# Graph network on one core: the softmax layers' edge loop keeps node columns, and W1 is applied in the node stage

## What is computed

```python
def _genconv(x, src, dst, W1, b1, g, be, W2, b2):
    msg = jax.nn.relu(x[src]) + EPS_MSG
    out = _softmax_aggregate(msg, dst, n) + x      # weights exp(msg), normalised per dst
    h = out @ W1 + b1                              # 128 -> 256
    mu = h.mean(axis=0)
    var = h.var(axis=0)                            # over all nodes
    h = (h - mu) * jax.lax.rsqrt(var + EPS_BN) * g + be
    h = jax.nn.relu(h)
    return h @ W2 + b2                             # 256 -> 128
```

## Time and profile before

| what | value |
|---|---|
| time, median of 3 runs | 6036.46 us (6026.17 to 6037.29) |
| span of the profiled execution | 6114.5 us (no time of its own is given beside it) |
| mean granted clock of TensorE | 0.846 |
| busy: PE, PEld, DVE, ACT, POOL | 69%, 58%, 39%, 31%, 55% |
| edge loops of layers 0, 1, 2 | 1324.60, 1299.00, 1246.00 us |
| stretch ahead of each loop | 68.40, 65.00, 67.00 us |
| node phase and table stores, layers 0, 1 | 66.00, 65.00 us |

### The profile page before, as it was taken

The page is one execution under the profiler, slowest core; times in us unless marked ns, Lnnn a source line. Parts: engine busy times, 40 slices in busy tenths (PEclk is TensorE's granted clock), DMA queues, the critical chain, the costliest instruction groups (busy, mean ns, idle before and its releaser), DMA issues.

```text
span 6114.5 us, 110249 instructions
## 1 busy us (share of the span) xinstructions
PE 4222.2 (69%) x26763; PEld 3555.3 (58%) x26763; DVE 2375.0 (39%) x6918; ACT 1871.9 (31%) x5164; POOL 3344.9 (55%) x3446
## 2 busy tenths in 40 slices
PE   2777777777677777777565555555556877777777
PEld 1666676766466666666455555555444655655555
DVE  3233333334333333333422222222533555555555
ACT  1222222222333333333321121111333444444445
POOL 1556665554366666666256666666135555555551
PEclk9888888888798888888777777777768989999999
DMA  2122222221233333333211111111134444444442
GB/s 69 51 61 62 61 61 61 61 62 44 59 104 105 104 103 104 103 105 104 61 36 43 43 42 43 43 43 44 52 93 122 124 116 123 121 118 123 118 122 73
DMA packets 389331, 487.68 MB, mean 80 GB/s; under 512 B 131848, under 2 KB 282106, under 8 KB 389224
## 3 DMA queue, kind: packets, MB, share of 16 engines
q0 software_dynamic: 119808, 245.58, 16.1%
q1 hardware_dynamic: 263161, 237.73, 12.8%
q10 hardware_dynamic: 6255, 3.20, 0.2%
HBM read 402.97 MB, written 83.21 MB: 80 GB/s over the span
## 4 chain that ended last, share of the span: by engine, by line
PE 21%; another core or an unknown queue 20%; issue 16%; ACT 7%; DVE 5%; DVEq 3%; ACTq 2%; DMA 1%; SPq 1%; PEldq 0%
PE ps L966 7%; PE ps L950 2%; DVEq L808 2%; PE ps L1422 1%; ACTq L808 1%; PE ps L1391 1%; PE ps L1410 1%; DVE xT L1496 1%; ACT work L896 1%; PE ps L1439 1%; PE ps L1428 1%; ACT work L1457 1%; ACT xT L1469 1%; PE ps L1152 1%
## 5 line engine op out<-in xcount | busy, mean ns | idle before, releaser
L782 POOL DMA_INDIRECT ring<-msg_table,idx_ring x2496 | 2437.6, 977 | 1669.2 <-issue 806.2
L966 PE MATMUL ps<-onehot,ring 128*128 128x128 f32 x9984 | 1542.0, 313 | 421.8 <-issue 378.0
L966 PEld LDWEIGHTS ps<-onehot,ring 128*128 128x128 f32 x9984 | 1423.3, 225 | 503.5 <-issue 449.5
L879 ACT ACTIVATE acc<-ps,b 128x42 f32 x1248 | 300.7, 292 | 2904.6 <-DMA starts<-in_dst 1871.2
L782 POOL DMA_INDIRECT ring<-h_table,idx_ring x832 | 831.0, 999 | 613.5 <-issue 205.9
L950 PE MATMUL ps<-work,W 128*128 128x128 f32 x2496 | 470.3, 317 | 299.1 <-DVE work L1024 179.0
L950 PEld LDWEIGHTS ps<-work,W 128*128 128x128 f32 x2496 | 415.3, 226 | 350.9 <-DVE work L1024 158.0
L992 DVE SCALAR_TENSOR_TENSOR ring<-ring 128x512 f32<-128x512 f32 x624 | 404.2, 648 | 449.3 <-ACT ring L884 324.6
L884 ACT ACTIVATE ring<-ring,negc 128x512 f32<-128x512 f32 x624 | 448.5, 719 | 0.0
L1017 DVE TENSOR_TENSOR work<-work,ps 128x84 f32<-128x84 f32 x624 | 151.6, 243 | 716.0 <-DMA msg_table<-ring 347.6
L1422 PE MATMUL ps<-work,few 128*128 128x512 f32 x416 | 245.1, 672 | 205.0 <-ACT work L1474 174.7
(11 more groups left out here) (193 smaller groups left out, 5658.2 us busy)
## 6 DMA issues: line engine op xcount, KB each, us to landing
e_few<-spare SPq DMA_DIRECT2D x208, 256.0 KB
xT<-e_few SPq DMA_DIRECT2D x208, 256.0 KB
work<-in_edge_attr SPq DMA_DIRECT2D x414, 128.0 KB
ring<-msg_table,idx_ring POOLq DMA_INDIRECT x2496
spare<-rel_rows SPq DMA_DIRECT2D x208, 126.0 KB
ring<-h_table,idx_ring POOLq DMA_INDIRECT x832
window<-h_parts SPq DMA_DIRECT2D x624, 15.8 KB
h_parts<-ring SPq DMA_DIRECT2D x75, 93.8 KB
```

The lines of the kernel that those rows point to most:

```text
L782: e.indirect_dma_start(out=dst[:, s, j, :], out_offset=None, in_=table, in_offset=bass.IndirectOffsetOnAxis(ap=idx_ring[:, s, j:j + 1], ax ...
L879: ins = e.activation(hid[:, h, bass.ds(w, W)], ps[2 + k.off % 2][:, 256 + h * P:256 + h * P + W], ACT.Identity, bias=b1[:, h:h + 1])
L966: ins = e.matmul(bank[:, k * P:(k + 1) * P], rows[:, s, j, :], onehot[:, s, j, :], start=(j == 0), stop=(j == J - 1))
```

## The change

- ACT no longer handles windows in the loop (L879 is gone, with its value_load). Ahead of the loop it copies all of x into `acc[:, 0]` in one instruction of 6250 columns (`kept`, L843 of the changed kernel), where before PE and ACT ran 25 blocks through W1.
- PE has no W1 in the edge phase. `e0` moves to the end of the step and uses only bank `ps[4]`, so that it waits for DVE's read of the group before; `e0_sums` and `few_e0` are a group later, in banks 5 and 6; the transposes no longer wait for ACT's windows.
- DVE writes quotient + x straight into `acc[:, 0]` at the group's window, two groups later than before. In its step, `acc` of group i - 2 now comes first, ahead of `mexp(i)`, the one-hot matrix is made a group ahead, and `er` or `e0T` is that of group i - 2. One value_load serves both window uses.
- The node phase begins with W1 over all columns: PE over `acc[:, 0]` in 25 blocks through five banks, ACT adds b1 into `hid`, and DVE's statistics follow block by block.
- POOL's and SP's programs are as before, other than in the semaphore counts. The fallback path is changed to match.

```diff
@@ -864,175 +839,145 @@
 
             def act(e, S):
                 first_indices(e, S)
-                e.wait_ge(S("params"), 16 * 6)
-                hidden_columns(e, S)
-                e.wait_ge(S("hid"), NCH)
-
-                def step(i):
-                    if (i - 4).inside(NG):
-
-                        k = i - 4
-                        w = window_start(e, k)
-                        wait(e, S("Wnode"), k)
-                        wait(e, S("hid_w"), k - 1)
-                        for h in range(2):
-                            ins = e.activation(hid[:, h, bass.ds(w, W)], ps[2 + k.off % 2][:, 256 + h * P:256 + h * P + W],
-                                               ACT.Identity, bias=b1[:, h:h + 1])
-                        ins.then_inc(S("hid_w"), 1)
+
+                e.activation(acc[:, 0, 0:N], xT, ACT.Copy).then_inc(S("kept"), 1)
+
+                def step(i):
                     if i.inside(NG):
                         gathered(e, S, i, layer)
                         e.activation(ex[:, i.off % RING, :, :], msg[:, i.off % RING, :, :], ACT.Exp,
                                      bias=negc[:, :]).then_inc(S("exp"), 1)
                         next_indices(e, S, i)
...
+                    if term and (i - 4).inside(NG):
+                        k = i - 4
+                        wait(e, S("few_e0"), k)
+                        wait(e, S(f"term_out{k.off % 4}"), k, 4, -4 * (k.off % 4))
+                        e.activation(term_out[k.off % 4], ps[5 + k.off % 2][:, :], ACT.Copy).then_inc(S("term"), 1)
                 pipeline(e, NG, RING, 2 * RING if term else RING, 4, step)
 
             def pe(e, S):
-                def without_edges(i):
-
-                    wait(e, S("hid"), i - 2)
-                    for h in range(2):
-                        ins = e.matmul(ps[i.off % 2][:, h * 256:h * 256 + CH], W1[:, h * P:(h + 1) * P], xT[:, cols(i)],
-                                       start=True, stop=True)
-                    ins.then_inc(S("W1"), 1)
-                e.wait_ge(S("params"), 16 * 6)
-                pipeline(e, NCH, 2, 2, 0, without_edges)
-                e.wait_ge(S("hid"), NCH)
-
...
-                    if attr and (i - 1).inside(NG):
-                        k = i - 1
-                        wait(e, S("eaT"), k)
-                        wait(e, S("er"), k - 2)
...
+                            pair = ea[i.off % 4][:, 2 * h:2 * h + 2, :].rearrange("p j c -> p (j c)")
+                            ins = e.transpose(ps[2 + i.off % 2][:, h * P:(h + 1) * P], pair, ident[:, :])
+                        ins.then_inc(S("ea_turned"), 1)
...
+                    if attr and (i - 3).inside(NG):
+                        k = i - 3
+                        wait(e, S("er"), k)
+                        wait(e, S("agg0"), k - 2)
+                        for j in range(J):
+                            ins = e.matmul(ps[5 + k.off % 2][0:HALF, 0:P], er[k.off % RING][:, j, :],
+                                           onehot[:, k.off % RING, j, :], start=(j == 0), stop=(j == J - 1))
+                        ins.then_inc(S("e0_sums"), 1)
+                    if term and (i - 3).inside(NG):
+                        k = i - 3
                         wait(e, S("e0T"), k)
                         wait(e, S("term"), k - 2)
                         for t in range(2):
-                            ins = few0_of(e, ps[6 + k.off % 2], t, e0T[k.off % RING])
+                            ins = few0_of(e, ps[5 + k.off % 2], t, e0T[k.off % RING])
                         ins.then_inc(S("few_e0"), 1)
-                    if (i - 3).inside(NG):
-                        k = i - 3
-                        wait(e, S("node"), k)
-                        wait(e, S("hid_w"), k - 2)
-                        for h in range(2):
-                            ins = e.matmul(ps[2 + k.off % 2][:, 256 + h * P:256 + (h + 1) * P], W1[:, h * P:(h + 1) * P],
-                                           node[k.off % 2], start=True, stop=True)
-                        ins.then_inc(S("Wnode"), 1)
...
                     if i.inside(NG):
+                        s, bank = i.off % RING, ps[i.off % 2]
+
                         wait(e, S("mexp"), i)
+                        wait(e, S("onehot"), i)
                         wait(e, S("acc"), i - 2)
...
+                    if both and (i - 1).inside(NG):
+                        k = i - 1
+                        wait(e, S("eaT"), k)
+                        wait(e, S("er" if attr else "e0T"), k - 1)
+                        if attr:
+                            for h in range(J // 2):
+                                ins = e.matmul(ps[4][:, h * P:(h + 1) * P], eaT[k.off % 2][:, h * P:(h + 1) * P],
+                                               ew0_pair[:, :], start=True, stop=True)
+                        else:
+                            ins = e.matmul(ps[4][:, 0:2 * P], ew0_pair[:, :], eaT[k.off % 2], start=True, stop=True)
+                        ins.then_inc(S("e0"), 1)
                 pipeline(e, NG, RING, RING, 3, step)
...
-                def step(i):
-                    if i.inside(NG):
-                        s = i.off % RING
-                        wait(e, S("sums"), i - RING)
-                        if attr:
-                            wait(e, S("e0_sums"), i - RING)
-                        make_onehot(e, i).then_inc(S("onehot"), 1)
...
+                def step(i):
+                    if i.base is None and i.off == 0:
+                        onehot_of(i)
                     if (i - 2).inside(NG):
+
                         k = i - 2
-                        wait(e, S("acc"), k)
-                        e.reciprocal(aggr[k.off % 4], sums[k.off % 4][:, 0, 0:W]).then_inc(S("quot"), 1)
-                    if i.inside(NG):
...
-                    if (i - 2).inside(NG):
...
-                    if attr and (i - 1).inside(NG):
-                        k = i - 1
-                        wait(e, S("e0"), k)
...
-                    if (i - 1).inside(NG):
-
-                        k = i - 1
                         by = e.value_load(shifts[0:1, bass.ds(k.times(1), 1)], min_val=0, max_val=W)
                         wait(e, S("sums"), k)
                         wait(e, S("acc"), k - 1)
                         new = ps[k.off % 2][:, 0:2 * P].rearrange("p (k w) -> p k w", k=2)[:, :, 0:W]
                         e.tensor_tensor(sums[k.off % 4][:, :, 0:W], sums[(k.off - 1) % 4][:, :, bass.ds(by, W)], new,
                                         ALU.add).then_inc(S("acc"), 1)
+                    if i.inside(NG):
+                        s = i.off % RING
+                        wait(e, S("exp"), i)
+                        e.scalar_tensor_tensor(out=msg[:, s, :, :], in0=msg[:, s, :, :], scalar=EPS_MSG,
+                                               in1=ex[:, s, :, :], op0=ALU.add, op1=ALU.mult).then_inc(S("mexp"), 1)
+                    if i.base is not None or i.off + 1 < NG:
+                        onehot_of(i - -1)
                     if (i - 2).inside(NG):
                         k = i - 2
+                        wait(e, S("acc"), k)
+                        e.reciprocal(aggr[k.off % 4], sums[k.off % 4][:, 0, 0:W]).then_inc(S("quot"), 1)
+                    if attr and (i - 2).inside(NG):
+                        k = i - 2
+                        wait(e, S("e0"), k)
+                        e.tensor_scalar(er[k.off % RING], ps[4][:, 0:J * HALF].rearrange("p (j c) -> p j c", j=J), 0.0, None,
+                                        ALU.max).then_inc(S("er"), 1)
...
+                    if (i - 2).inside(NG):
+                        k = i - 2
+                        t = aggr[k.off % 4]
+                        wait(e, S("quot"), k, 2, 1)
+                        e.tensor_tensor(t, t, sums[k.off % 4][:, 1, 0:W], ALU.mult).then_inc(S("quot"), 1)
+                    if (i - 4).inside(NG):
+                        k = i - 4
                         w = window_start(e, k)
+                        if attr:
+                            wait(e, S("e0_sums"), k)
+                            wait(e, S("agg0"), k - 1)
+                            place = Z0[0:HALF, bass.ds(w, W)]
+                            e.tensor_tensor(place, place, ps[5 + k.off % 2][0:HALF, 0:W], ALU.add).then_inc(S("agg0"), 1)
+                        if k.base is None and k.off == 0:
+                            e.wait_ge(S("kept"), 1)
                         wait(e, S("quot"), k, 2, 2)
-                        wait(e, S("Wnode"), k - 2)
-                        e.tensor_tensor(node[k.off % 2][:, 0:W], aggr[k.off % 4], xT_all[:, bass.ds(w, W)],
+                        wait(e, S("node"), k - 1)
+                        e.tensor_tensor(acc[:, 0, bass.ds(w, W)], aggr[k.off % 4], xT_all[:, bass.ds(w, W)],
                                         ALU.add).then_inc(S("node"), 1)
-                    if attr and (i - 3).inside(NG):
-                        k = i - 3
```

(22 more changed lines are left out.)

109 lines of the change are left out of this document (26 added, 83 removed).

## The result

The changed kernel takes **5899.33 us** (median of 4 runs, 5886.68 to 5905.97) beside 6032.16 for the kernel before in the same series: a ratio of 0.9779, 95% interval 0.9765 to 0.9793. It is 133 us faster. The forecast was 5580, a gain of 456, more than three times what came. The time lies above the forecast's own 5328 to 5803, and 11 us inside the stated 5160 to 5910, whose upper end was drawn to take in rival (b). It is within 10 us of (b), 5892, but the reasons lie between (b) and (d).

The account below looks back on a forecast made before the run. PE's late results while POOL gathers were taken to bound the edge loops. Prologue 174 plus loops 314 less node stage 30 made 458 off 6036.5, so 5580 us; range 5160 to 5910, the forecast's own 5328 to 5803.

Parts of the forecast that it names:

- rival (b): Edge loops keep their pace, set by the late hand-off to POOL and DVE; only the prologue goes: 5892 us, chance 0.20.
- (d): Prologue's time comes back in the loops, whose ring starts empty: 120 of 174, less some 20; near 5990, chance 0.05.
- The bounding view: Edge loops: PE's results reach other engines several us late while POOL gathers without a break, at once when it pauses.
- Part one, the prologue: Ahead of each layer's loop: without the 25 blocks, 58 us saved in each layer, 174 in all.
- Part two, the loop: Edge loops: without the round PE to ACT to PE, 5.7 us a group in all layers, gaining 314 us.
- g: Edge loops: a round through PE and back while POOL gathers; 7.46 us in layer 0 before, 5.4 to 6.9 after.
- The two-rate formula: Edge loops: a group's time T follows from 5.04/g + (T - 5.04)/u = 1, with 5.04 us of gathers a group.
- u: Edge loops: a round through PE and back while POOL pauses; 4.11 us before the change, 3.5 after.
- the upper T: Edge loops: a group's time at the long hand-off of 5.9 us: 6.0 us, which gives 5803 us for the kernel.
- The clock: Layers 0 and 1: falling to layer 2's clock costs up to 0.5 us a group; a quarter taken, inside the 5.7.
- Part three, the node stage: Node stage: W1 ahead of the statistics adds 10 us a layer, 30 in all; it could be 5 or 20.
- Rival (c): Layers 0 and 1: e0's single bank makes every group wait, 7.8 us a group; slower, 6452 us, chance 0.08.

Follow-up runs that it names:

- e0: A code name, PE's product in bank 4; its run gave the changed kernel two banks (4 and 7) for it: 5903.62 us late, 4998.69 prompt.

## Why the prediction failed, step by step

- **The bounding view.** That PE's results are late while POOL gathers, read from the timeline and not from the page's busy shares, was right: where they are prompt the same kernel takes 4994. The size was not: 7.5 and 7.0 us were single readings from the long end, and the "mean hand-off" of 4.4 was a remainder; L879's mean over the trace is 2.74. And I took the lateness for a property of the program. It comes with the placement, and that the kernel before could be 1040 us faster unchanged was in no rival.
- **Part one, the prologue.** The stretch fell by 57 to 61 us in each layer, 58 forecast. The step that failed is "until the last column was through, nothing else of the layer ran": POOL had gathered eight groups, and the loop lived on them. 174 was the term, 88 is its size. Rival (d) named the mechanism, 120 less some 20 of the 174 coming back, and was given 0.05; the loops' 103 us of the two traces are near it.
- **Part two, the loop.** The step that failed is the round that sets g. I divided 7.46 us into 3.0 of work and 4.4 of hand-off as if one round, PE to ACT to PE, set the pace, and then shortened the work. Two banks for e0 changed nothing, no transposes 0.06 us a group, four banks 0.04. The wait went from L879 to L855, a round I had not listed: transposes, ACT's copy, e0. With that taken away it stayed on ACT. My reading is that one release frees all that wait for PE, so that shortening one round gives only what it adds to that; no run shows it by itself. The gain forecast was 314; it is 113 where both kernels start with an empty ring. What sets the pace of a late loop in place of a single round stays open.
- **The two-rate formula.** What was wrong is g after the change, 5.4 to 6.9. Read backwards from 6.18 with u = 3.5 it is 7.5, as before the change; that is a fit with one free number and proves nothing of the form. That a loop is POOL's gathers plus its pauses the traces do show: the pauses over 0.4 us after the first exponentials are 304.7, 268.7 and 237.3 us before and 252.8, 231.5 and 165.5 after, or 1.2, 1.1 and 0.8 us a group where 0.7 was forecast; in the prompt trace of the kernel before they are 2.3 us in all. One slip in the sum: 8.65 - 2.03 - 0.83 is 5.8 and not 5.9, which makes the upper T 5.95 in place of 6.0 and changes nothing here.
- **The clock.** Layers 0 to 2 had 0.86, 0.83 and 0.70 where 0.87, 0.88 and 0.74 stood: a little lower; the prediction had allowed for that inside the 5.7. The layers of one trace agree with the rule of the Trainium skill (TensorE: Matmul & The Clock Gate, "Part 1: The HAM clock gate"), that activity releases the throttle: 0.86 where PE is busy 985.10 of 1287 us, 0.70 where it is 589.53 of 1232. Across placements the busy share does not tell it: with two banks for e0, prompt, layer 0 had 1.00 with PE busy 775.03 of 1061 us. No experiment held the clock, so its share of the loop is open.
- **Part three, the node stage.** 30 us forecast for three layers; 32 within one series (7.2 to 12.7 a layer), 46 in the two traces of the first comparison: right. The rows show ACT's pairs at 0.83 as assumed, and 13.30 us ahead of the first, in which the loop's last steps drain and the phases meet:

```profile
1433.13 0.83 ACT L1082 ACTIVATE acc<-ps,b 128x250 f32<-128x250 f32 x2 [13.30 <-PE ps L1103]
...
1436.47 9.86 ACT L1082 ACTIVATE acc<-ps,b 128x250 f32<-128x250 f32 x23 [0.84 <-PE ps L1103]
```

- **Rival (c)**, the single bank slower: did not come, and two banks in place of one change nothing. **Rival (b)**'s time came by a sum of other terms: neither did the loops keep their pace, nor is the prologue worth 174.
- **Profile against median.** The trace of before is 78 us longer than its median and outside all four timed runs, and the two traces differ by 210 us where the medians differ by 133. Some 18 of the 210 lie in the edge layers, which the change leaves alone. Sums from stages of the first two traces overstate the gain; those above from one series (169 for 164) close better.

## What to carry to other kernels

Before a stretch ahead of a loop is priced in full, ask what the bounding engine has piled up in it: a ring that is filled meanwhile gives its time back in the loop. When several engines wait for one source and all are freed within a us, shortening one round may only move the wait to the next; take a step out of the chain on trial before the gain is put into a sum. Before one row of a timeline is put into a sum, look at the same distance in its neighbours. And run the kernel before beside every experiment: here two placements of one kernel were 21 to 23% apart, ten times the change.

## What the runs showed of the hardware

- The unchanged kernel took 6032, 6038.81 and 6144.38 us in some series and 4991 to 4995 in others. What differs is when PE's results reach ACT, DVE and POOL: from L950's end to L879's start 0.12 us in the median and 0.22 in the mean prompt, 1.75 and 2.74 late and up to 13.8, while the gathers' own durations (1000 and 977 ns) differ little and stages without gathers take the same. Signals into PE come in 0.06 us (DVE's L1024 to L950) in the late trace too. What in the placement does it no run shows; each of the two late chips on record was seen once.
- Late results go with a run of gathers on POOL (299 of 518 hand-offs over 2 us in a run, 4 of 105 in a pause). At a run's end PE passes ready matmuls 0.72 us apart, at the full granted clock. Neither the gathers' bytes (an eighth of them left the pace at 5.90) nor any single round of the program that was tried explains it; whether the number of gathers does was not tried where results are late.
- Twelve semaphore increments on POOL between groups of gathers cost nothing that a measurement shows (1.0001, 0.9991 to 1.001); three drains cost 2.5 us a group (6536.55 us).
